# The mix over channels as one plain fp32 matmul, in a four-layer fp32 kernel on one core

## The reference

```
x = x + ssm_conv(x, K) * mask          # K [32, 512] from the SSM parameters, causal convolution over time, by FFT
x = x + einsum('bct,bcd->bdt', x, W1[cond])     # cond[b] in 0..15, W1, W2 are [16, 32, 32]
x = x + einsum('bct,bcd->bdt', x, W2[cond])
x = x + lora_mlp(x)                    # silu(x Wg + lora) * (x Wu + lora), times Wd + lora; 512 -> 1376 -> 512
```

## Time and profile before

| | |
|---|---|
| median of 3 runs | 1116.83 us (1113.99, 1116.83, 1116.93) |
| time of the profiled execution | 1114.27 us |
| its span, first to last instruction | 1112.4 us |
| mean granted TensorE clock | 0.983 |
| TensorE matmul busy | 1040.5 us (94%), 6176 records |
| TensorE weight load busy | 935.1 us (84%) |
| ScalarE / GpSimd / VectorE busy | 441.7 / 528.8 / 297.2 us |

### The profile page before, as it was taken

How to read it: one execution, slowest core, us unless ns; L and a number is a source line. 1 busy time by engine, 2 the same in 40 slices (tenths; PEclk the granted TensorE clock), 3 DMA queues, 4 the chain that set the end, 5 groups by cost and what they waited for, 6 DMA issues and landing times.

```text
span 1112.4 us, 19314 instructions
## 1 busy us (share of the span) xinstructions
PE 1040.5 (94%) x6176; PEld 935.1 (84%) x6176; DVE 297.2 (27%) x550; ACT 441.7 (40%) x691; POOL 528.8 (48%) x334
## 2 busy tenths in 40 slices
PE   3577389999999999999999999999999999999997
PEld 3567368899998888889988999988898899889996
DVE  8576212222222222212222222222222122222222
ACT  7544143433344344433344333443444333443331
POOL 0587285444544454544554445545454445444441
PEclk9899789999999999999999999999999999999999
DMA  9687444343424242433333343424243333334320
GB/s 341 224 302 265 148 123 117 99 121 99 121 88 130 64 141 74 132 94 106 102 104 113 90 127 91 121 81 133 65 137 89 113 106 101 104 98 119 106 65 19
DMA packets 100921, 135.52 MB, mean 122 GB/s; under 512 B 26339, under 2 KB 59364, under 8 KB 100900
## 3 DMA queue, kind: packets, MB, share of 16 engines
q1 hardware_dynamic: 99380, 133.35, 39.9%
q10 hardware_dynamic: 1520, 1.92, 0.6%
HBM read 118.21 MB, written 16.99 MB: 122 GB/s over the span
## 4 chain that ended last, share of the span: by engine, by line
PE 93%; DVE 3%; issue 1%; ACT 1%; DMA 1%; SPq 0%; POOL 0%; DVEq 0%; ACTq 0%; POOLq 0%
PE ps L979 45%; PE ps L1021 25%; PE ps L989 7%; PE ps L948 6%; PE ps L1010 3%; PE ps L963 2%; PE ps L969 1%; DVE us_lo L787 1%; PE ps L1034 1%; PE ps L1033 1%; PE ps L997 1%; SPq L188 0%; PE ps L1002 0%; ACT wd_hi L483 0%; DVE xs L701 0%
## 5 line engine op out<-in xcount | busy, mean ns | idle before, releaser
L979 PE MATMUL ps<-wg_hi,x_hi 128*128 128x512 f32 (+2 forms) x768 | 296.6, 386 | 1.7 <-DVE x_lo L832 1.7
L979 PE MATMUL ps<-wg_lo,x_hi 128*128 128x512 f32 (+2 forms) x768 | 290.9, 379 | 0.0
L979 PE MATMUL ps<-wg_hi,x_lo 128*128 128x512 f32 (+2 forms) x768 | 290.7, 379 | 0.0
L444 POOL TENSOR_TENSOR bst<-braw,bst 128x1024 fp32r<-128x1024 f32 (+1 forms) x96 | 213.8, 2227 | 106.7 <-ACT bst L573 106.7
L589 ACT ACTIVATE at_hi<-ps 128x512 fp32r<-128x512 f32 (+1 forms) x96 | 54.1, 563 | 302.6 <-PE ps L1010 301.1
L979 PEld LDWEIGHTS ps<-wg_hi,x_lo 128*128 128x128 f32 x768 | 144.6, 188 | 25.6
L979 PEld LDWEIGHTS ps<-wg_hi,x_hi 128*128 128x128 f32 x768 | 144.9, 189 | 24.0 <-issue 2.1
L979 PEld LDWEIGHTS ps<-wg_lo,x_hi 128*128 128x128 f32 x768 | 145.0, 189 | 21.6
L1021 PE MATMUL ps<-wd_hi,at_hi 128*128 128x288 f32 (+1 forms) x704 | 155.3, 302 | 1.4 <-DVE at_lo L855 1.4
L1021 PE MATMUL ps<-wd_hi,at_lo 128*128 128x288 f32 (+1 forms) x704 | 150.9, 296 | 0.0
L1021 PE MATMUL ps<-wd_lo,at_hi 128*128 128x288 f32 (+1 forms) x704 | 150.3, 295 | 0.0
(11 more groups left out here) (142 smaller groups left out, 1275.4 us busy)
## 6 DMA issues: line engine op xcount, KB each, us to landing
braw<-in_tb SPq DMA_DIRECT2D x256, 128.0 KB, 2.7
braw<-in_tb SPq DMA_DIRECT2D x128, 96.0 KB, 2.4
adraw<-in_tad SPq DMA_DIRECT2D x128, 88.0 KB, 2.0
ur<-in_xT SPq DMA_DIRECT2D x16, 512.0 KB, 4.2
x1p<-yo SPq DMA_DIRECT2D x16, 512.0 KB, 3.3
x_raw<-x1p SPq DMA_DIRECT2D x32, 256.0 KB, 2.7
xb<-in_x SPq DMA_DIRECT2D x32, 256.0 KB, 2.9
agraw<-in_ta SPq DMA_DIRECT2D x128, 64.0 KB, 2.0
```

Source lines behind the costliest of these rows:

```text
L444: sub(v, b_from(p, q), v.bitcast(F32), ALU.subtract).then_inc(s["blo"], 1)
L979: last = mm(bank[:, 0:n], x3s[a][:, k, :], wgs[b][:, k, o:o + n], start=(k == 0 and a + b == 0), stop=False, skip_group_check=True)
```

## The change

The mix reads `xa` itself and plain fp32 mix weights, as one matmul call. The high and low copies of the sum and of the mix matrices go, with their semaphores. `wbd` and `tm_d` are half as large, and the tile `x1_hi` is gone, so the tiles that are allocated behind them stand at other addresses.

```diff
-    tm_d = nc.dram_tensor("tm_d", (NCOND, C, 2, C), F32, kind="Internal").ap()
+    tm_d = nc.dram_tensor("tm_d", (NCOND, C, C), F32, kind="Internal").ap()
...
-        wbd = sb("wbd", [P, 2, 2, P], F32R)
+        wbd = sb("wbd", [P, 2, P])
...
-        wms = sb("wms", [C, NCOND, 2, C])
+        wms = sb("wms", [C, NCOND, C])
...
-        x1_hi, xa, x1_lo = split_buffers("x1", [P, T])
-        x1s = [x1_hi, x1_lo]
+        xa = sb("xa", [P, T])
...
-            sp.wait_ge(s["wms"], 2)
-            sp.dma_start(tm_d.rearrange("s c l d -> c s l d"), wms[:]).then_inc(s["tst"], 16)
+            sp.wait_ge(s["wms"], 1)
+            sp.dma_start(tm_d.rearrange("s c d -> c s d"), wms[:]).then_inc(s["tst"], 16)
...
-                    sp.dma_start(wbd[p0:p1, p, :, p0:p1].bitcast(F32), tm_d[e[b]].rearrange("a c l d -> (a c) l d")
+                    sp.dma_start(wbd[p0:p1, p, p0:p1], tm_d[e[b]].rearrange("a c d -> (a c) d")
...
-            def x1_low(t):
-                pool.wait_ge(s["x1hi"], t + 1)
-                sub(x1_lo[:], xa[:], x1_hi[:].bitcast(F32), ALU.subtract).then_inc(s["x1lo"], 1)
...
-            def x1_high(t):
-                act.wait_ge(s["xsum"], t + 1)
-                copy(x1_hi[:], xa[:], ACT.Copy).then_inc(s["x1hi"], 1)
...
-            dve.wait_ge(s["wms"], 1)
-            V.tensor_tensor(wms[:, :, 1, :].bitcast(F32R), wmp.rearrange("c (s d) -> c s d", d=C),
-                            wms[:, :, 0, :], ALU.subtract).then_inc(s["wms"], 1)
...
             def mix(t, p):
-                pe.wait_ge(s["x1lo"], t + 1)
+                pe.wait_ge(s["xsum"], t + 1)
                 pe.wait_ge(s["wbd"], (t + 1) * 16 * GB)
-                for n, (a, b) in enumerate(PASSES):
-                    last = mm(misc, wbd[:, p, a, :], x1s[b][:], start=(n == 0), stop=(n == 2))
+                last = mm(misc, wbd[:, p, :], xa[:], start=True, stop=True)
                 last.then_inc(s["x3mm"], 1)
```

More of the change, by code:

```diff
@@ L165, in cond_resid_kernel @@
             ev0 ev1 ev2 ev3 yst0 yst1 done wz msk
-            xin xsum x1hi x1lo wbd x3mm x3n x3t x3hi x3lo
+            xin xsum wbd x3mm x3n x3t x3hi x3lo
             ag aghi aglo ad adhi adlo b0 b1 bhi blo bd bdhi bdlo
@@ L395, in _ @@
             nc.gpsimd.memset(zer[:], 0.0).then_inc(s["zer"], 1)
-            nc.gpsimd.memset(wbd[:].bitcast(F32), 0.0).then_inc(s["wz"], 1)
+            nc.gpsimd.memset(wbd[:], 0.0).then_inc(s["wz"], 1)
             def w_low(n):
@@ L450, in _ @@
             x_sum(0)
-            x1_low(0)
             ag_low(0)
@@ L463, in tile_lows @@
                     ag_low(t + 1)
-                    x1_low(t + 1)
                 b_low(t, p, 2)
@@ L503, in _ @@
             wm3 = wmp.rearrange("c (s d) -> c s d", d=C)
-            nc.scalar.activation(wms[:, :, 0, :].bitcast(F32R), wm3, ACT.Copy).then_inc(s["wms"], 1)
+            nc.scalar.activation(wms[:], wm3, ACT.Copy).then_inc(s["wms"], 1)
             w_high(range(1, 7))
@@ L597, in td_high @@
                 copy(tds[0][:], misc[:, 0:P], ACT.Copy).then_inc(s["tdhi"], 1)
-            x1_high(0)
             ag_high(0, True)
@@ L618, in tile_act @@
                     ag_high(t + 1)
-                    x1_high(t + 1)
                 b_high(t, p, 2, t * 3 + 1)
```

## The result

| | before | after |
|---|---|---|
| median | 1116.93 us (11 runs, 1113.99 to 1119.44) | 1119.29 us (11 runs, 1118.9 to 1121.33) |
| profiled execution | 1114.27, span 1112.4 | 1118.9, span 1117.1 |
| its mean granted clock | 0.983 | 0.984 |

The ratio is 1.0024, 95% interval 1.0014 to 1.0033. The medians are 2.36 us apart (interval 1.6 to 3.7). That the change makes the kernel slower therefore rests as well on the tiles of the trace, each of which is longer. At 0.24% it stays under the 0.3% at which the prediction drew its line.

The account below looks back on a forecast made before the run. TensorE, saturated in the token-tile loop, was taken to bound the kernel. Loop +4.9, first tile -0.75 and preparation 0 made +4.15 us on the 1115.9 us mean: 1120.1 us, range 1117 to 1123.5.

Parts of the forecast that it names:

- The place: Token-tile loop: TensorE never rests, so any change in its stream's length changes the kernel's time by the same amount.
- Two records a call, two cycles a column, 858 ns: Mix on TensorE: one plain fp32 call is two weight loads and two matmuls, 858 ns against 0.70 us.
- Four cycles a column: Rival on the mix's streaming rate: 1.71 us a mix, +31 us in all, 1147 us; chance 0.04.
- one cycle: Rival on the mix's streaming rate: 0.46 us a mix, -8.2 us with the start, 1107.7 us; chance 0.05.
- Relief of ScalarE and GpSimd is worth nothing in the loop: Loop: removing the copy (0.64 us) and subtraction (1.28 us) per tile gains nothing, as TensorE's stream covers both.
- The weight load: Mix on TensorE: a plain fp32 weight load of 139 ns lies hidden under a matmul of 427 ns and adds nothing.
- +0.158 a tile, +4.9 in all: Loop: the longer mix adds 0.158 us in each of 31 saturated tiles, +4.9 us, bounds +4.7 and +5.9.
- Addresses: Rival: tiles moved by 1 KB a partition shift the loop 3 us either way; chance 0.09, shared with other small shifts.
- The first tile, "I take -0.75, bounds -0.7 and -2.0": First tile's serial chain: first chunk about 1.5 us earlier, worth 0.75 us if the clock returns at the same moment.
- The rival of a start that gives back 2 us: First tile: clock returns earlier or first layers move further, giving back 2.0 us, total +2.9, 1118.8 us; chance 0.22.
- Preparation, 0 +- 0.5: Before the convolution: removed subtraction gains nothing; earlier ur loads may cost or gain, 0 with 0.5 us either way.
- the likeliest case: Whole kernel: the forecast itself, longer loop mix less the start's gain, 1118.5 to 1122.5 us; chance 0.60.

Follow-up runs that it names:

- mix_twice: The kernel after with each plain fp32 mix matmul issued twice, the second overwriting the first; 1147.77 us, ratio to the kernel before 1.0271.
- chain_kept: The kernel after with ScalarE's copy and GpSimd's subtraction still done into an unread tile, the mix waiting for them; 1122.24 us, ratio to before 1.0041.
- mix_halves: The kernel after with each mix made as two calls of 256 columns; single execution, 1121.26 us.
- first_plain: The kernel before with one plain fp32 mix, without copy and subtraction, in the first tile only; 1115.72 us, ratio 0.9986.
- before_again: The kernel before, unchanged, run again under another label; 1115.82 us, ratio 0.9988.
- after_again: The kernel after, unchanged, run again for a second trace; single execution, 1119.66 us.

## Why the prediction was right, and where it was off

**The place.** "TensorE's stream is saturated in the loop, so whatever lengthens it lengthens the kernel": shown. The tiles of after differ in the mix, no PE wait appears, and the second mix of mix_twice adds its whole 0.86 us to every tile.

**Two records a call, two cycles a column, 858 ns**: shown, by 64 records, 0.86 in the chain, 1.72 for two calls, 0.87 for four half ones. Four cycles a column (1.71 us) and one cycle (0.46) are both excluded. (For one cycle the prediction's line at 0.62 us a mix adds up to -3.2 and not -3.4; nothing hangs on it.) The Trainium skill ("FP8 and Floating Point Precision", TensorE Precision Notes) gives a true fp32 product four passes; the measured 0.86 us agrees with four times 0.213. The halving for FP32_LOW_HIGH in the Trainium skill ("Perfetto Trace Analysis", Engine Utilization) fits each of the two records and not the call, if that is the mode they run in, which no row names.

**Relief of ScalarE and GpSimd is worth nothing in the loop**: shown by chain_kept, which has that work and the same loop.

**The weight load** was mis-sized, 192 ns for 139, without effect, since it lies under a matmul as assumed; mix_halves shows that even 213 ns cover it.

**+0.158 a tile, +4.9 in all**, was a little too much: +0.133 and +4.12. The mix itself is right. The chunk behind it takes 2.79 or 2.78 instead of 2.80, the LoRA matmuls 0.91 instead of 0.93, which I had not counted. Why is open. It isn't the relieved engines (chain_kept has both fast figures). The 0.01 of the chunk goes with the plain mix in all five traces that have it in the loop. The 0.02 of the LoRA matmuls doesn't: mix_twice and mix_halves have 0.93. Paces also differ where no edit changes the work: another four LoRA matmuls of the tile take 0.94 us in before, after and first_plain and 0.92 in chain_kept, mix_twice and mix_halves. Addresses, which the rival with a chance of 0.09 names, were not tried. If it is they, they bore 0.8 us, and not the 3 us that I had priced.

**The first tile, "I take -0.75, bounds -0.7 and -2.0"**, is the step that was off. The mechanism up to the first chunk was right in each link: no copy, no subtraction, a mix of 2.08, ScalarE held by braw, 1.45 to 1.55 us gained (8.52 and 8.51 against 7.07 and 6.96). I then halved it, on the thought that the clock would come back at the same moment as before. The windows of after:

```profile
145.75:149.50 3.75, 3.75 (x10) 3.12 (x11) 0.00 (x0) 0.99 (x1) 3.75 (x2) 0.50 0.49 140
149.50:153.40 3.90, 2.97 (x19) 2.62 (x17) 0.85 (x2) 0.91 (x2) 3.90 (x3) 1.00 0.58 168
```

In before the clock came back 3.5 us behind the first chunk's start (145.23, then 148.7), in after 3.75 us behind it (145.75, then 149.50). Counted from the start of the sum it is 12.0 in before, 14.1 in before_again and 12.6 in chain_kept, which have the long chain, and 10.8 in after, 11.7 in after_again and 11.4 in first_plain, which have the short one (those of before and after read off, the others worked out from the mean clock of a window across the change). Counted from the start of the first chunk the two groups don't differ: 3.5, 5.6 and 3.6 us with the long chain, 3.75, 4.7 and 4.2 with the short one. And the stretch at half clock that ends there began at 124.8, 129.2 and 130.7 in the first group and at 129.0, 130.2 and 129.4 in the second, so it lasted 23.9 us in each execution with the long chain and 20.5 in each with the short one. So it comes earlier with the chunk, and on average the gain is kept. That rests on three traces each. From chunk to LoRA matmul the two traces of before took 7.58 and 8.46 us, the two of after 7.64 and 8.13: no loss of 0.75 to be seen, within a spread of 0.9 that is as large as what I look for. The medians say the same: 4.12 - 1.5 = +2.6 is what the trace gives, +2.36 the medians. The rival of a start that gives back 2 us had the right sign with its chance of 0.22; about 1.5 of the 2 us came.

**Preparation, 0 +- 0.5**: not contradicted. SP stood behind less: the ur loads went out at 33.21 instead of 34.68. ScalarE then waited 2.21 us for tr, and the first convolution matmul came at 40.10 and 40.01, against 39.88 and 40.53. A difference below the spread of 0.65 can't be told.

**The sum** was +4.15 and came out as +2.36. The 1.8 us between are 0.8 of the loop and 0.7 of the start; the rest, 0.3, is within the spread of the medians (interval 1.6 to 3.7 us). The time of 1119.29 lies inside the range of 1117.0 to 1123.5 and inside the 1118.5 to 1122.5 of the likeliest case, for the reason given there: a longer mix in a saturated stream, less what the start gives back. But the claim that it would be slower by over 0.3%, with its chance of 0.58, did not come true: the two mis-sized terms took it to 0.24%, on the other side of a line that lay 0.8 us from my forecast.

## What to carry to other kernels

A plain fp32 product costs 0.86 us for 512 columns, three fp32r products 0.70 (both at full clock): in a stream that TensorE bounds, the three are cheaper, and the splits they need are free as long as other engines have room. At the start, where nothing is covered, the one call saves two links of a serial chain, so decide by stage and not for the whole kernel; and read a gain ahead of a slow-clock stretch together with the moment at which the clock returns, which may move with it. The prices are those of 128 x 128 weights with 512 columns; the accuracy of the two ways was not compared. Where an effect is near 0.1%, run the unchanged kernel again as a variant of its own before believing it, and compare distances inside the trace, not absolute times.

## What the hardware showed beyond expectation

- The recorded clock reads 1.00 early in a trace while 512-column matmuls are 0.43 us apart, twice the 0.213 of full speed. Within one row of chain_kept the pace of 32-column records goes from 53 to 29 ns under a recorded 1.00.
- A 128-column weight load of plain fp32 took 192 ns for the mix and 139 ns for transposes of the same type and size; the mix's equals that of the fp32r matmuls (188).
- With 47 matmuls without use ahead of and inside the thin stretch, the first chunk was shorter, from between 6.3 and 7.3 us to 4.5, though the clock still fell between.
- The time from sum to LoRA matmul varied by 0.87 us between two executions of the same code, all of it behind the first chunk's start.
